# The query matrices absorbed on the keys' side: one shared query, keys per head, scores in two passes

## What is computed

```python
c_q = h_t @ W_DQ + b_DQ            # 32 per token
c_kv = h_t @ W_DKV + b_DKV         # 32 per token
q_c = (c_q @ W_UQ + b_UQ)          # 8 heads x 128
k_c = (c_kv @ W_UK + b_UK)
v_c = (c_kv @ W_UV + b_UV)
q_r = (c_q @ W_QR + b_QR)          # 8 heads x 32
k_r = (h_t @ W_KR + b_KR)          # one, for all heads
scores = (q_c . k_c + q_r . k_r) / sqrt(160)
attn = softmax(scores); o = attn @ v_c; return o @ W_O + b_O
```

## Time and profile before

| | |
|---|---|
| time, median of 3 runs | 2651.54 us (2647.05 to 2657.14) |
| span of the profiled execution | 2654.2 us |
| TensorE busy | 2460.8 us, 93% |
| VectorE busy | 2076.5 us, 78% |
| ScalarE busy | 1634.0 us, 62% |
| GpSimd busy | 725.5 us, 27% |
| mean granted TensorE clock | 0.967 of full |

### The profile page before, as it was taken

The page is one execution under the profiler, slowest core; times in us unless marked ns, Lnnn a source line. Parts: engine busy times, 40 slices in busy tenths (PEclk is TensorE's granted clock), DMA queues, the critical chain, the costliest instruction groups (busy, mean ns, idle before and its releaser), DMA issues.

```text
span 2654.2 us, 67343 instructions
## 1 busy us (share of the span) xinstructions
PE 2460.8 (93%) x26752; PEld 1794.7 (68%) x26752; DVE 2076.5 (78%) x3553; ACT 1634.0 (62%) x2872; POOL 725.5 (27%) x601
## 2 busy tenths in 40 slices
PE   4999999999999999999999999899998999999998
PEld 2667657676677766777667676676765767667765
DVE  3959879688786887778877778778788697796976
ACT  2758457575576655766566755667556584575845
POOL 1211342204422052220522215112152022520135
PEclk7999999999999999999999989999999998999989
DMA  6110221102111031110211112010121101211021
GB/s 238 34 37 13 76 68 41 38 5 92 52 41 40 2 108 37 43 38 26 87 33 49 33 42 80 28 50 29 57 68 32 49 21 61 68 34 48 18 72 64
DMA packets 93370, 136.25 MB, mean 51 GB/s; under 512 B 10111, under 2 KB 55240, under 8 KB 92552
## 3 DMA queue, kind: packets, MB, share of 16 engines
q1 hardware_dynamic: 84872, 115.16, 13.4%
q0 software_dynamic: 8192, 16.79, 2.1%
HBM read 101.31 MB, written 30.61 MB: 50 GB/s over the span
## 4 chain that ended last, share of the span: by engine, by line
PE 57%; DVE 20%; issue 14%; ACT 6%; POOL 2%; DVEq 0%; ACTq 0%; POOLq 0%
PE ps L1399 9%; PE ps L1537 7%; DVE neg_max L1061 7%; PE ps L1477 6%; DVE probsT L1076 5%; PE ps L1577 5%; PE ps L1406 4%; ACT probs L722 4%; PE ps L1562 4%; PE ps L1628 4%; PE ps L1499 3%; PE ps L1420 2%; DVE ffn L1204 2%; PE ps L1372 2%; PE ps L1488 2%
## 5 line engine op out<-in xcount | busy, mean ns | idle before, releaser
L722 ACT ACTIVATE probs<-ps,neg_max 128x1024 f32<-128x1024 f32 x512 | 571.7, 1117 | 157.0 <-DVE neg_max L1061 154.8
L1061 DVE TENSOR_REDUCE neg_max<-ps 128x1 f32<-128x1024 f32 x512 | 623.3, 1217 | 30.4 <-PE ps L1537 19.2
L1537 PE MATMUL ps<-keys,q_parts 64*128 64x512 f32 x3072 | 507.0, 435 | 37.1 <-ACT probs L722 35.6
L1399 PE MATMUL ps<-q_parts,w_split 128*128 128x512 f32 x1536 | 469.9, 443 | 17.3 <-ACT ffn L771 9.6
L1562 PEld LDWEIGHTS ps<-ident,probs 64*128 64x128 f32 x8192 | 342.5, 141 | 122.1 <-ACT probs L722 53.2
L620 POOL TENSOR_TENSOR probs<-ffn,q_parts 128x512 f32<-128x512 f32 x208 | 297.5, 1433 | 385.4 <-DMA q_parts<-gate_rows 152.7
L1399 PEld LDWEIGHTS ps<-q_parts,w_split 128*128 128x128 f32 x1536 | 288.8, 193 | 165.2 <-issue 62.8
L1562 PE MATMUL ps<-ident,probs 64*128 64x64 f32 x8192 | 348.9, 226 | 40.1 <-ACT probs L722 36.0
L1537 PEld LDWEIGHTS ps<-keys,q_parts 64*128 64x128 f32 x3072 | 257.8, 190 | 178.8 <-ACT probs L722 83.2
L1076 DVE COPY probsT<-ps 128x512 f32<-128x512 f32 x512 | 348.8, 681 | 20.7 <-PE ps L1562 18.5
L1577 PE MATMUL ps<-probsT,latent 128*32 128x128 f32 x8192 | 327.8, 279 | 16.9 <-DVE o_latent L1054 11.4
(11 more groups left out here) (217 smaller groups left out, 3279.0 us busy)
## 6 DMA issues: line engine op xcount, KB each, us to landing
w_split<-w_parts SPq DMA_DIRECT2D x132, 256.0 KB, 2.6
q_parts<-gate_rows SPq DMA_DIRECT2D x64, 512.0 KB, 4.1
y_rows<-probs SPq DMA_DIRECT2D x40, 256.0 KB, 2.2
x_in<-in_x SPq DMA_DIRECT2D x9, 512.0 KB, 4.3
w_parts<-q_parts SPq DMA_DIRECT2D x2, 2048.0 KB, 13.7
out<-x_mid SPq DMA_DIRECT2D x8, 512.0 KB, 3.2
ffn<-in_gate_up SPq DMA_DIRECT2D x1, 2048.0 KB, 9.1
probsT<-in_gate_up SPq DMA_DIRECT2D x1, 2048.0 KB, 13.4
```

The source lines that it names most:

```text
L722: nc.scalar.activation(probs[:, t % 3, :], banks(2 * (t % 2)), ACT.Exp, bias=neg_max[:, t % 4:t % 4 + 1], accum_out=row_sum[:, g % 2, t % ...
L1061: nc.vector.tensor_reduce(neg_max[:, t % 4:t % 4 + 1], banks(2 * (t % 2)), X, ALU.max, negate=True).then_inc(max_ready.sem, 1)
L1399: mm = nc.tensor.matmul(ps[:, bank, :], w_split[:, f % CHUNK_SLOTS, h, k * P:(k + 1) * P], tokens[:, half], start=(part == 0), stop=(part ...
L1537: mm = nc.tensor.matmul(ps[:, 2 * (t % 2) + c, :], q_parts[rows, j, q, n * P:(n + 1) * P], keys[rows, k, :], start=(part == 0), stop=(part ...
```

## The change

The matrices that turn the 32-wide query latent into a head's query move to the keys. There is one query for all heads: the query latent c_q, four copies on the 128 partitions. Each head has its own key of 32 rows: `w_absorb` times the old key ("key base"). What the query biases add is one number a key and head (`beta`), made by one small product for all heads, stored to DRAM and loaded back as two more rows (high and rest) beside the keys' low parts, against ones in the query.

Since a head's key needs only 32 rows, the three products of parts fit into two passes of 64 rows: (query high, query low) against (key high, key high), and (query high, ones) against (key low, beta). Six matmuls of scores become four, with the same number of columns each.

Where the work stands now:

- The shared query is made at unit 15 of the dense experts (`queries`, L1473), and rounded in three ScalarE instructions (L725 on 128 rows, L729 twice on 32 rows, 1024 columns each); VectorE subtracts on 32 rows at its units 15 and 16 (L965).
- The key base is made at unit 17, beta at unit 19. Four later flow steps move by two units (`FLOW_KV` to `FLOW_PROJ`).
- Keys of heads 0 to 3: one matmul each after gate and up of the last unit (`next_heads`). Keys of heads 4 to 7: beside blocks 8, 11, 14 and 17 (`LATE_HEADS`). For each head ScalarE rounds 128x512 (L735) and VectorE subtracts 32x512 twice (L974).
- The queries at the starts of the quads are gone.

```diff
-NEXT_KEYS = 29
+NEXT_QUERIES = 15
+NEXT_KEYS = 17
+NEXT_BETA = 19
+RUN_BANKS = (6, 7, 2, 3)
+LATE_HEADS = {8: 4, 11: 5, 14: 6, 17: 7}
...
-FLOW_KV = 20
-FLOW_OUT = 22
-FLOW_HEADS = 25
-FLOW_PROJ = 28
+FLOW_KV = 22
+FLOW_OUT = 24
+FLOW_HEADS = 27
+FLOW_PROJ = 30
...
+            def queries_round(b, bank):
+
+                act.wait_ge(query_mm.sem, query_mm.at(b, 1))
+                nc.scalar.activation(query_a[:, :], banks(bank), ACT.Identity, bias=b_dq[:, :]
+                                     ).then_inc(query_high.sem, 1)
+                for c in range(2):
+                    rows = slice(2 * DC * c, 2 * DC * c + DC)
+                    nc.scalar.activation(query_b[rows, :], banks(bank)[rows, :], ACT.Identity, bias=b_dq[rows, :]
+                                         ).then_inc(query_high.sem, 1)
...
+            def queries_rest(bank, c):
+
+                dve.wait_ge(query_high.sem, query_high.at(b, 1))
+                rows = slice(2 * DC * c + DC, 2 * DC * (c + 1))
+                nc.vector.scalar_tensor_tensor(query_a[rows, :], banks(bank)[rows, :], b_dq[rows, :],
+                                               query_a[rows, :].bitcast(F32), ALU.add, ALU.subtract
+                                               ).then_inc(query_low.sem, 1)
+
+            def head_rest(h, bank, k):
+
+                dve.wait_ge(head_high.sem, head_high.at(b, k))
+                for c in range(2):
+                    rows = slice(2 * DC * c, 2 * DC * c + DC)
+                    nc.vector.tensor_tensor(key_low[rows, h % QUAD, :], ps[rows, bank, :], key_high(h)[rows, :].bitcast(F32),
+                                            ALU.subtract).then_inc(head_low.sem, 1)
...
-                    for h in heads_of(w):
-                        dve.wait_ge(q_high.sem, q_high.at(b, h + 1))
-                        nc.vector.scalar_tensor_tensor(
-                            q_parts[:, h % QUAD, 1, :], banks(2 * (h % QUAD)), b_q[:, h:h + 1],
-                            q_parts[:, h % QUAD, 0, :].bitcast(F32), ALU.add, ALU.subtract).then_inc(q_ready.sem, 1)
-                        if h == 0 and index > 0:
-                            experts_add(Sequence(index - 1))
+                    if w == 0 and index > 0:
+                        experts_add(Sequence(index - 1))
...
-                    for part, (q, k) in enumerate(((0, 0), (0, 1), (1, 0))):
+                    for part, (q, k) in enumerate(((query_a, key_high(h)), (query_b, key_low[:, h % QUAD, :]))):
                         for c, rows in enumerate(STRIPS):
-                            mm = nc.tensor.matmul(ps[:, 2 * (t % 2) + c, :], q_parts[rows, j, q, n * P:(n + 1) * P],
-                                                  keys[rows, k, :], start=(part == 0), stop=(part == 2))
+                            mm = nc.tensor.matmul(ps[:, 2 * (t % 2) + c, :], q[rows, n * P:(n + 1) * P],
+                                                  k[rows, :], start=(part == 0), stop=(part == 1))
...
+                    if u == NEXT_QUERIES:
+                        pe.wait_ge(qnT_ready.sem, qnT_ready.at(b, 2))
+                        pe.wait_ge(sums2_taken.sem, sums2_taken.at(b, 1))
+                        queries(b, 6)
+
                     if u == NEXT_KEYS:
+                        pe.wait_ge(query_high.sem, query_high.at(b, 3))
+                        pe.wait_ge(query_low.sem, query_low.at(b, 2))
+                        key_projection(b)
```

More of the change, by code:

```diff
@@ L282, in two_layer_kernel @@
         y_rows = nc.dram_tensor("y_rows", (ROWS, D), F32, kind="Internal").ap()
-        xs_parts = [q_flat[:, h * 4 * SEQ:h * 4 * SEQ + ROWS] for h in range(2)]
+        xs_parts = [shared[:, 2 * SEQ + h * 2 * BANK:2 * SEQ + (h + 1) * 2 * BANK] for h in range(2)]
         ys = probs[:, :, :].rearrange("p a b -> p (a b)")[:, 0:ROWS].rearrange("p (j d) -> p j d", d=D)
@@ L643, in _ @@
             act.wait_ge(raw_in[1].sem, 16)
-            for i in range(2):
-                nc.scalar.copy(w_prep[:, i, :, 0, :], w_raw[1][:, 8 * i:8 * i + 8, :]).then_inc(prep_high.sem, 1)
+            for i, piece in enumerate(W_PIECES):
+                nc.scalar.copy(w_prep[i][:, :, 0, :], w_raw[1][:, piece, :]).then_inc(prep_high.sem, 1)
             act.wait_ge(raw_in[0].sem, 16)
@@ L1381, in gates_transpose, with experts @@
                 mm.then_inc(gateT_mm.sem, 1)
-            def experts(b, beside, next_queries):
+            def experts(b, beside, next_heads):
                 def gate_up(u):
@@ L1523, in _ @@
             transpose_norm(None, 0, 6)
-            key_projection(None)
+            queries(None, 0)
             latents(None, 5, range(NT))
             router(None, 0, 5, NT * DC)
+            key_projection(None)
+            beta_products(None)
+            pe.wait_ge(beta_ready.sem, beta_ready.at(None, 1))
+            for h in range(QUAD):
+                head_keys(h, RUN_BANKS[h])
             for index in range(BATCH):
```

339 lines of the change are left out of this document (213 added, 126 removed).

## The result

The changed kernel takes 2702.56 us (median of 4 runs, 2694.92 to 2709.73); the kernel before, on the same chip, 2653.14 (4 runs, 2647.05 to 2657.14). The ratio is 1.0186, 95% interval 1.0161 to 1.0212: slower by 1.9%. Forecast: 2687, range 2640 to 2706.

What follows compares the result with a forecast made beforehand. VectorE was taken to pace most tiles, TensorE those of the second quad's first half. Eight times 5.7, seven times (1.4 - 3.3) and +3 once gave +35: span 2689.5, less 2.7, 2687 us; 8-in-10 range 2640 to 2706.

Steps and rivals of the forecast that it cites:

- The dense chain: Dense experts, units 15 to 18: roundings delay clamp, low part, key product and unit 18; +7.9 us a batch, clock +2.5.
- 32 rows: Query roundings and low parts: operations on 32 partitions cost no less than on 128; 0.7 us per 512-column key piece.
- half-price bound: Dense chain's lower end: if 32 rows cost half, two roundings and one low part save 1.6 us, leaving +6.3.
- second rival, The stall is short and the clock holds: Unit 17: cheap 32-row operations (+6.3 us) and no low clock spell; 2654 us, no change; chance 0.20.
- The quads: Second quad's first half: tiles go from 2.02 to 1.85 us, 1.7 us saved; elsewhere VectorE covers the shorter scores.
- Blocks and first quad: Chosen experts' blocks and first quad: predicted stage differences of -1.5 and -1.9 us.
- little over 1 us: Start of the first quad, seven times: the first maximum can start at 710.7, a little over 1 us earlier.
- the start of the program: Before the first batch: beta rows' store and reload, doubled product chain and clearing of low keys; about +3 us once.
- The chain is hidden: Unit 17: TensorE finds the low part ready at the key product; 76 us less, 2611 us; chance 0.10.
- The clock falls in the quads too: Both quads: shorter scores leave TensorE idle, two more low spells a batch; 26 us more, 2713 us; chance 0.10.

Runs made afterwards that it cites:

- fill: Changed kernel with unit 18's gate and up products done three times over in TensorE's idle time before the key product at unit 17: 2677.16 us, ratio 1.0086.
- Spread: Changed kernel with the three query roundings moved to units 16, 17 and 18, behind each SiLU, key product at unit 19, beta at 21: 2651.89 us, ratio 0.9995.
- short: Changed kernel with the two 32-row query roundings doing 16 columns instead of 1024: 2668.52 us, ratio 1.0057.
- later: Changed kernel with roundings over units 16 to 18, reordered program start, heads 2 and 3 rounded first, and key product at unit 20, beta 22: 2604.31 us, ratio 0.9819.

## Why the prediction was right, and which term was off

- **The dense chain.** Right in place, order and size. Predicted 7.9 + 2.5 + 0.3 a batch, measured 11.35. Part by part, the smaller products aside: unit 18 moved by 9.0 without the clock (9.0 foreseen); the key product and unit 18 lost 2.5 to the clock on average (2.5 foreseen, bounds 0 and 4; "fill" gave 2.0 back); last gate and up to the end of the last down product 9.4 us instead of 8.1, +1.3 (+1.4). "Spread", "short" and "fill" take away the roundings' delay, 1.7 us of it, and the clock alone; between units 17 and 31 they give back 5.5 us (8 expected, a wait of 1.94 is left), 2.2 (1.7) and 2.0 (2.6). That the parts come out within some tenths is partly luck: the low spell at the start of the stage alone differs by more among kernels with the same code there.
- **A small part that was left out:** that of the interplay. In "short" the chain was priced alone, with its clock penalty unchanged; a shorter wait also shortened the low spell, by 3.0 us, worth 0.6 us a batch.
- **32 rows.** The forms' mean: rows 729, 965 and 974 of the code against the earlier trace rows.

```profile
L965 DVE SCALAR_TENSOR_TENSOR query_a<-ps,b_dq,query_a 32x1024 fp32r<-32x1024 f32 x18 | 23.1, 1285 | 19.3 <-ACT query_a L725 19.0
...
L729 ACT ACTIVATE query_b<-ps,b_dq 32x1024 fp32r<-32x1024 f32 x18 | 19.7, 1096 | 0.2
...
L974 DVE TENSOR_TENSOR key_low<-ps,shared 32x512 fp32r<-32x512 f32 x128 | 87.3, 682 | 42.6 <-ACT shared L735 39.8
```

A quarter of the partitions costs 1285 against 1279 ns and 1096 against 1114; the half-price bound, on which the second rival stood, is out. 682 for 512 elements is the 0.7 I took.

- **The quads.** Right: only the first half of the second quad gains. There the tiles are 1.81 us apart on average (1.85 foreseen), and VectorE is now the bound in them. The stage's gain was 3.7 (3.2 foreseen). VectorE of after:

```profile
541.43 0.68 DVE L1174 COPY probsT<-ps 128x512 f32<-128x512 f32 x1
542.02 1.21 DVE L1164 TENSOR_REDUCE neg_max<-ps 128x1 f32<-128x1024 f32 x1
543.15 0.68 DVE L1174 COPY probsT<-ps 128x512 f32<-128x512 f32 x1
543.75 1.21 DVE L1164 TENSOR_REDUCE neg_max<-ps 128x1 f32<-128x1024 f32 x1
```

- **Blocks and first quad.** -1.2 and -1.6 where -1.5 and -1.9 stood. The maximum's "little over 1 us" of lead was 1.3.
- **The term that was mis-sized: the start of the program,** "about +3 once", measured 11.6. Of these 3.9 lie before the tokens are normalized: the doubled chain of small products (64 of them from 26.85 to 34.75) and the copies of the absorbed matrices on VectorE. The other 7.7 lie behind the first transposes: the beta product with its two roundings, four head keys partly at the low clock (5.62 us; eight matmuls at the full clock take 3.4), and eight low parts in a row. VectorE of after:

```profile
70.69 1.76 DVE L1003 MEMSET key_low<- 128x2048 f32 x1 [0.38 <-issue]
73.24 1.40 DVE L974 TENSOR_TENSOR key_low<-ps,shared 32x512 fp32r<-32x512 f32 x2 [0.79 <-ACT shared L735]
74.80 4.26 DVE L974 TENSOR_TENSOR key_low<-ps,shared 32x512 fp32r<-32x512 f32 x6 [0.16 <-ACT shared L735]
```

The first maximum starts at 79.09, behind the last low part. The clearing, which the prediction counts, holds nothing up: VectorE waits 0.79 us for ScalarE's rounding behind it. Nor does the way of the beta rows through DRAM: the first scores that read them start at 76.26, with no idle time, and the maximum could have come then. The prediction gave one sum for this place and no working; at the very start the new steps stand one behind the other. With this term right the forecast would have been 2696. The stages came to 38.7 us where 32 were summed, 5 of the difference in the dense experts.
- **The rivals.** "The chain is hidden" was made true only by "later", where the roundings no longer stand before the clamp and the key product has three more units of lead: 2604 us with its other two edits, where 2611 stood under that rival. "The stall is short and the clock holds" fell with the 32-row operations. "The clock falls in the quads too" was half right: the low level lasts 7.4 us a batch more in the first quad and 2.5 in the second, but both stages became shorter all the same, since VectorE or the routing arithmetic sets their pace. By the Trainium skill, "TensorE: Matmul & The Clock Gate" (section "A second HAM failure mode: psum-queue depth-cycling"), short idle times between groups make the clock swing; the trace agrees for the starts of the quads, not for a steady stretch (1.00 above), and where the page has the throughput suffer, the quads became shorter (69.09 and 60.08 us against 70.72 and 63.80). What its section "HAM oscillation — how this bites in real kernels" has longer gaps do is what after shows at unit 17, and "fill" shows that the low spell goes with the idle time.

## What to carry to other kernels

A block of elementwise work moved into a busy stage costs least by its own duration and most by what is queued behind it: here 3.2 us of roundings between exp and a clamp became 5.9 us of new idle time on TensorE and 2.5 of low clock. The same instructions one by one, each behind its unit's SiLU and with the key product three units later, cost nothing that could be measured: a dense stage of 133.39 us against 133.93 before. Place the producer, its roundings and the consumer so that each has a whole unit of slack, and move the consumer behind the next unit's products, which need nothing from it. When a wait on TensorE can't be avoided, price the clock with it, and look for work to put into it.

## What was not expected of the hardware

- Useless matmuls in an idle stretch paid: 144 of them, some 35 us of TensorE work in all (8 x 4.34, 672.63 to 676.97 in one batch), and the kernel became 25 us faster, 16 of them at this place. An idle time of 2.74 us ahead of them was followed by no low spell in the batch shown and in four others, and by one of 3.4 us in three; the same 2.74 us in the run with the key product at unit 18 was followed by one in six of eight batches, over unit 18 (2.72 us instead of 1.50).
- The clock is low for a long or a short while at the start of the program in kernels whose code up to there is the same, and this moves the first exponential by some 4 us. What decides between them stays open.
- The low clock rose from 3.8 to 11.2 us in each first quad without making it longer. A mean granted clock (0.937 after, 0.967 before) tells little until one knows which stage it is low in.
- The low clock ahead of unit 8 of the dense experts lasts 8.5 to 11.9 us a batch in kernels whose code there is the same. A stage total from one trace carries this; what an edit is worth is read from the stretch where it acts.
